# A weight stage in which each product waits for its own loads, and the first rows of x join it

## The reference

```
Q, K = x @ W_Q.T, x @ W_K.T;  invQ, invK = Q @ W_inv.T, K @ W_inv.T
xV  = einsum('btd,kdr->btkr', Q_side, V)          # forward: Q, V_fwd; inverse: invQ, W_inv_exp
yW  = einsum('btd,kdr->btkr', K_side, W)          # forward: K, W_fwd; inverse: invK, V_inv
h   = gelu(Q_side @ router_w1.T + router_b1);  weights = softmax(h @ router_w2.T + ...)
out = einsum('btkr,kdr->btd', xV * cumsum(yW) * weights, U) + weights @ b;  (fwd + alpha * inv) @ W_O.T
```

## Time and profile before

| | us |
|---|---|
| median of 3 runs | 2596.01 |
| the three runs | 2595.65, 2611.66, 2596.01 |
| profiled execution, its time | 2596.03 |
| profiled execution, its span | 2594.4 |
| PE busy, share of the span | 2275.7, 88% |
| DVE busy | 1828.6, 70% |
| ACT busy | 1465.8, 56% |
| first product on PE starts at | 27.67 |

### The profile page before, as it was taken

One profiled execution on the slowest core, in us unless ns is written; L12 is line 12 of the kernel. 1 busy time (PEld: TensorE's weight loads), 2 busy tenths in 40 slices (PEclk: granted clock), 3 DMA queues, 4 the chain that ended last, 5 costly groups with the idle time before them and its releaser, 6 DMA issues. The chain is left out here.

```text
span 2594.4 us, 45262 instructions
## 1 busy us (share of the span) xinstructions
PE 2275.7 (88%) x15192; PEld 1266.4 (49%) x15192; DVE 1828.6 (70%) x3199; ACT 1465.8 (56%) x2211; POOL 442.8 (17%) x647
## 2 busy tenths in 40 slices
PE   4678589999999999999999999859999967799988
PEld 3456233333333333333333333238888856555568
DVE  2554689999999999999999999313333356677936
ACT  2343167777777777777777777722222222255643
POOL 0000000000000000000000000013333310255645
PEclk9799589999999999999999999979999989576989
DMA  3666900220400403204004000042332259956465
GB/s 118 217 245 238 119 11 3 32 33 7 60 3 12 54 5 41 25 5 61 3 12 54 5 12 5 3 118 66 85 109 74 65 181 356 161 123 133 103 176 163
DMA packets 179609, 213.86 MB, mean 82 GB/s; under 512 B 71808, under 2 KB 121856, under 8 KB 176576
## 3 DMA queue, kind: packets, MB, share of 16 engines
q1 hardware_dynamic: 166576, 192.90, 30.2%
q10 hardware_dynamic: 7152, 13.84, 2.7%
q0 software_dynamic: 5728, 5.00, 0.9%
HBM read 121.41 MB, written 88.87 MB: 81 GB/s over the span
## 5 line engine op out<-in xcount | busy, mean ns | idle before, releaser
L931 DVE TENSOR_REDUCE a_maxes<-a_ps_a 128x2 f32<-128x1024 f32 x1024 | 1201.5, 1221 | 110.5 <-PE a_ps_a L1045 106.6
L996 ACT ACTIVATE a_prob<-a_ps_s 128x512 f32<-128x512 f32 (+1 forms) x1376 | 1035.7, 804 | 365.0 <-PE a_ps_s L1071 359.1
L1071 PE MATMUL a_ps_s<-a_Q,a_K 50*128 50x512 f32 x2048 | 593.9, 453 | 91.2 <-ACT a_prob L996 89.7
L1045 PE MATMUL a_ps_a<-a_K,a_Q 48*128 48x512 f32 x2048 | 550.8, 454 | 28.6 <-DMA a_Q<-s_halves 14.0
L1083 PE MATMUL a_ps_o<-a_prob,a_V 128*17 128x512 f32 x4096 | 540.9, 600 | 0.1
L1071 PEld LDWEIGHTS a_ps_s<-a_Q,a_K 50*128 50x128 f32 x2048 | 277.1, 185 | 508.5 <-ACT a_prob L996 457.9
L1045 PEld LDWEIGHTS a_ps_a<-a_K,a_Q 48*128 48x128 f32 x2048 | 245.2, 189 | 232.6 <-issue 104.9
L889 POOL DMA_DIRECT2D a_Q<-a_m_parts x128 | 64.3, 502 | 1282.7 <-DVE a_m_parts L923 1279.1
L1475 ACT ACTIVATE a_prob<-a_ps_s 128x512 f32<-128x512 f32 (+1 forms) x256 | 136.0, 583 | 134.1 <-PE a_ps_s L1566 131.0
L1416 DVE CUSTOM_DVE_ANT_0 a_scratch<-a_ps_a,k_mask 128x256 f32<-128x256 f32 (+1 forms) x512 | 177.4, 412 | 46.1 <-PE a_ps_a L1530 45.9
L1530 PE MATMUL a_ps_a<-a_K,a_Q 48*128 48x256 f32 (+1 forms) x512 | 128.5, 379 | 31.5 <-DMA a_Q<-s_halves 30.5
(11 more groups left out here) (177 smaller groups left out, 2327.6 us busy)
## 6 DMA issues: line engine op xcount, KB each, us to landing
s_halves<-p_parts SPq DMA_DIRECT2D x64, 512.0 KB, 5.0
s_xT<-p_xT SPq DMA_DIRECT2D x64, 256.0 KB, 4.3
c_xT<-s_xT SPq DMA_DIRECT2D x64, 256.0 KB, 4.8
a_K<-s_halves SPq DMA_DIRECT2D x63, 256.0 KB, 6.7
a_Q<-s_halves SPq DMA_DIRECT2D x186, 64.0 KB, 9.9
s_v<-p_v_out SPq DMA_DIRECT2D x16, 544.0 KB, 4.2
s_cT<-p_cT SPq DMA_DIRECT2D x32, 256.0 KB, 3.5
c_cT<-s_cT SPq DMA_DIRECT2D x32, 256.0 KB, 5.1
```

What stands on the lines that cost most here:

```text
L931: nc.vector.tensor_reduce(maxes[:, :, slot, qt, kc], ps_a[:, o:o + 2 * CH].rearrange("p (z k) -> p z k", z=2), AX.X, ALU.max).then_inc(a_d ...
L996: nc.scalar.activation(prob[:, ring:ring + len(t), :].rearrange("p r q -> p (r q)"), ps_s[:, bank:bank + len(t) * CH], ACT.Exp, scale=scal ...
L1045: last = nc.tensor.matmul(ps_a[:, o + side * CH:o + (side + 1) * CH], Q[rows, q0:q0 + P], K[rows, k0:k0 + CH], start=True, stop=True)
L1071: last = nc.tensor.matmul(ps_s[:, bank + x * CH:bank + (x + 1) * CH], K[rows, k0:k0 + P], Q[rows, q0:q0 + CH], start=True, stop=True)
```

## The change

The loads are put in eleven groups with a semaphore each, in another order, and the two first chunks of x (batch 0 and 1) are put between them. PE waits for the group of each product; the router's two products are made first. The plain splits are placed between the products' splits by a table, `PLAIN_AT`. The statistics of both chunks, the inverse roots and the normalising of the first are done in the weight stage; for this the buffers of the rows (`row_buffers`) live in a scope of their own around it and the projection of layer 0, and in one around that of layer 1, each closed by clearing its semaphores and a barrier. `row_statistics`, `inverse_root` and `normalise_rows` are the nested functions of `phase_project` word for word, moved out and given the buffers. What follows in layer 0 begins with the transposes.

```diff
@@ phase_weights
+        loads = {
+            "inverse": [(square["WinvT"][:], "W_invT"), (square["WQ"][:], "W_Q"), (square["WK"][:], "W_K")],
+            "router": [(square["W1T"][:], "router_w1T")],
+            "Vf": [(wide["Vf"][:], "V_fwd")], "Vi": [(wide["Vi"][:], "W_inv_exp")],
+            "qkv0": [(raw_qkv[:, 0], "w_qkvT_0")],
+            "Wf": [(wide["Wf"][:], "W_fwd")], "Wi": [(wide["Wi"][:], "V_inv")],
+            "o0": [(raw_o[:, 0], "w_oT_0")],
+            "out": [(square["WOT"][:], "W_OT"), (wide["Uf"][:], "U_fwd"), (wide["Ui"][:], "U_inv"),
+                    (bT[:, :, 0:E], "b_fwdT"), (bT[:, :, E:2 * E], "b_invT")],
+            "qkv1": [(raw_qkv[:, 1], "w_qkv_1")],
+            "last": [(raw_o[:, 1], "w_out_1"), (raw_g[:, :, 0:E1], "gateT"),
+                     (raw_g[:, :, E1:E1 + E1 * R1], "lora_UT"), (raw_g[:, :, E1 + E1 * R1:], "weightT"),
+                     (raw_v[:], "lora_V"), (W["w2"][:], "router_w2T")],
+        }
+        loaded = {g: n.sem(f"{g}_loaded") for g in loads}
...
+        base = E1 + E1 * R1
+        plain = [("qkv0", lambda part: W["qkv0"][:, part], raw_qkv[:, 0], 1.0),
+                 ("o0", lambda part: W["o0"][:, part], raw_o[:, 0], 1.0),
+                 ("qkv1", lambda part: W["qkv1"][:, part], raw_qkv[:, 1], 1.0),
+                 ("last", lambda part: W["o1"][:, part], raw_o[:, 1], 1.0),
+                 ("last", lambda part: W["gate"][:, part, :, 0:base], raw_g[:, :, 0:base], 1.0),
+                 ("last", lambda part: W["gate"][:, part, :, base:], raw_g[:, :, base:], 0.5),
+                 ("last", lambda part: W["loraV"][:, part], raw_v[:], 1.0)]
+        PLAIN_AT = {4: (0,), 8: (1,), 11: (2,), 13: (3, 4, 5, 6)}
...
-            for dst, src, k in loads:
-                sp.dma_start(dst, src.rearrange("(k p) n -> p k n", p=P)).then_inc(loaded, DMA)
+            for g, group in loads.items():
+                for dst, key in group:
+                    sp.dma_start(dst, I[key].rearrange("(k p) n -> p k n", p=P)).then_inc(loaded[g], DMA)
+                if g in ("router", "Vi"):
+                    load_rows(sp, L, I["x"], 0, 0 if g == "router" else 1)
...
+            def plain_high_part(i):
+                g, dst, src, factor = plain[i]
+                act.wait_ge(loaded[g], DMA * len(loads[g]))
+                nc.scalar.activation(dst(0), src, ACT.Copy, scale=factor).then_inc(plain_high, 1)
...
                 dst = split_target(W, j)
...
+                for i in PLAIN_AT.get(j, ()):
+                    plain_high_part(i)
...
-            act.wait_ge(loaded, DMA * n_loads)
-            for dst, src, factor in plain_splits(W, raw_qkv, raw_o, raw_g, raw_v):
-                nc.scalar.activation(dst(0), src, ACT.Copy, scale=factor).then_inc(high, 1)
...
-            pe.wait_ge(loaded, DMA * n_loads)
+            def have(g):
+                pe.wait_ge(loaded[g], DMA * len(loads[g]))
+            have("inverse")
...
+            have("router")
             j = 0
+            for t in range(DK):
+                for r, left in enumerate((WQ, WIQ)):
+                    for k in range(DK):
+                        o = (2 + j % 6) * CH + r * D
+                        last = nc.tensor.matmul(bank[:, o:o + D], left[:, k, t * P:(t + 1) * P],
+                                                square["W1T"][:, k, :], start=(k == 0),
+                                                stop=(k == DK - 1), skip_group_check=True)
+                last.then_inc(product, 1)
+                j += 1
             for left, right in ((WQ, "Vf"), (WIQ, "Vi"), (WK, "Wf"), (WIK, "Wi")):
...
+                have(right)
                 for t in range(DK):
...
+            have("out")
...
+            def plain_low_part(i):
+                g, dst, src, factor = plain[i]
+                dve.wait_ge(plain_high, i + 1)
+                nc.vector.scalar_tensor_tensor(dst(1), src, factor, f32(dst(0)), ALU.mult, ALU.subtract
+                                               ).then_inc(plain_low, 1)
+            row_statistics(nc, dve, L, 0, 0, passed)
             for j in range(N_SPLIT):
                 dve.wait_ge(high, 3 + j)
                 dst = split_target(W, j)
                 nc.vector.tensor_tensor(dst(1), bank[:, (2 + j % 6) * CH:(3 + j % 6) * CH], f32(dst(0)),
                                         ALU.subtract).then_inc(low, 1)
-            for i, (dst, src, factor) in enumerate(plain_splits(W, raw_qkv, raw_o, raw_g, raw_v)):
-                dve.wait_ge(high, 4 + N_SPLIT + i)
-                nc.vector.scalar_tensor_tensor(dst(1), src, factor, f32(dst(0)), ALU.mult, ALU.subtract
-                                               ).then_inc(low, 1)
+                for i in PLAIN_AT.get(j, ()):
+                    plain_low_part(i)
+                if j == 1:
+                    row_statistics(nc, dve, L, 0, 1, passed)
+                if j == 2:
+                    normalise_rows(nc, dve, L, 0, 0)
...
            dve.wait_ge(drawn, N_DRAWN)
...
+            dve.wait_ge(rows_loaded, DMA * len(rows))
...
+            for u in range(2):
+                inverse_root(pool, W, L, u, u)
...
+def row_buffers(n):
+    L = {"xn": n.sb("xn", [P, 2, TT, D]), "stats": n.sb("stats", [P, 2, TT, 6]),
+         "mean_var": n.sb("mean_var", [P, 2, TT, 2]), "var_eps": n.sb("var_eps", [P, 2, TT]),
+         "rstd": n.sb("rstd", [P, 2, TT]), "x_loaded": [n.sem(f"x_loaded{u}") for u in range(2)]}
+    for name in ("stat", "eps_ready", "rstd_ready", "xn_ready"):
+        L[name] = n.sem(name)
+    return L
+def load_rows(sp, L, x_dram, i, u):
+    sp.dma_start(L["xn"][:, u], x_dram[u, ds(i * CH, CH), :].rearrange("(t p) d -> p t d", p=P)
+                 ).then_inc(L["x_loaded"][u], DMA)
+def row_statistics(nc, dve, L, i, u, passed):
...
+def inverse_root(pool, W, L, c, u):
...
+def normalise_rows(nc, dve, L, i, u):
...
@@ phase_project
-            load(sp, 0, 0)
-            load(sp, 0, 1)
+            if not first:
+                load(sp, 0, 0)
+                load(sp, 0, 1)
...
-            statistics(0, 0)
-            statistics(0, 1)
-            normalise(0, 0)
+            if not first:
+                row_statistics(nc, dve, L, 0, 0, passed)
+                row_statistics(nc, dve, L, 0, 1, passed)
+                normalise_rows(nc, dve, L, 0, 0)
...
@@ recurrent_blocks
-            phase_weights(nc, W, I)
-            phase_project(nc, W, S, I["x"], 0)
+            with ExitStack() as first_projection:
+                L = row_buffers(Names(nc, first_projection, "l0"))
+                phase_weights(nc, W, I, L)
+                phase_project(nc, W, S, L, I["x"], 0)
             phase_attend_full(nc, W, S)
             phase_combine_experts(nc, W, S, I["x"], S["x1"])
-        phase_project(nc, W, S, S["x1"], 1)
+        with ExitStack() as second_projection:
+            L = row_buffers(Names(nc, second_projection, "l1"))
+            phase_project(nc, W, S, L, S["x1"], 1)
```

120 lines of the change are left out of this document (39 added, 81 removed).

## The result

| us | before | changed |
|---|---|---|
| median of the runs on one chip | 2595.83 (4 runs, 2589.51 to 2611.66) | 2563.43 (4 runs, 2549.81 to 2594.64) |
| all runs of this study | mean 2595.4, median 2596.8, deviation 9.9 (39 runs) | mean 2561.7, median 2558.8, deviation 12.8 (16 runs) |
| first product on PE starts | 27.67 | 8.36 |
| weight stage ends | 67.81 | 43.92 |
| first transpose | 78.47 | 45.08 |

The ratio is 0.9858 [0.9814, 0.9902]: the kernel is faster by 1.4%. That the two agree so closely is partly luck: a single run lies 10 to 13 us off its mean.

A forecast was written before the change was run, and what follows sets the result against it. PE, near 9 tenths busy through full attention, bounds the kernel, so the weight stage, where it waited 27.7 us for loads, only moves the start. -19.7 - 5.4 - 9.7 + 1.0 = -33.8 from 2596.03 gives 2562.2; range 2554 to 2574.

The forecast's parts named there:

- The first product: Weight stage: PE's first product waits for three loads only, starting at 8.0 instead of 27.67 us; gain 19.7 (17.2 to 21.3).
- The page's fit: Trainium skill's estimate for one transfer, 2 us plus bytes at 436 GB/s: first three loads there near 4.7 us; not adopted.
- Group waits, splits and rows, at 0: Weight stage: later load groups arrive in time, and splits and rows of x fit between the products; cost 0.
- The rival of starving products: Weight stage: real group waits make PE stand and run at half clock; gain falls to 8, 2588 us; 6%.
- the one of loads that don't land in the order of issue: Weight stage: Vf's group lands with the crowd near 30 us; gain 21.2, 2575 us; 7%.
- The margins: Weight stage: time between a group's landing and PE's need of it; smallest 5.7 us, for Vf.
- The tail: Weight stage's end: less work stays behind the last product, so it ends at 62.42, not 67.81; gain 5.4 us (4.5 to 5.8).
- The head: Start of the next stage: rows of x already normalised, so PE transposes when the barrier opens; gain 9.7 us (8.5 to 9.8).
- Barriers: End of each projection: one more clear and barrier, 0.5 us each, +1.0 in all (0.8 to 1.7).
- a run's own scatter: Range of the total: 2 us or so for this, plus shifts of the projection's clock dips, widened the forecast case to 2554 to 2570.
- the attention takes a different time from its first key load to its end: Full attention: one of the listed signs that the prediction is wrong; PE clock there was expected unchanged.
- the slower rival: Attention's opening: PE's clock rises later, 9.3 us lost per 10 us of such work; about 2655 us for 100 us; 4%.

The follow-up runs named there:

- experiment 5: Changed kernel with ACT issuing its ten rows of biases only after the three first loads have landed; 2571.15 us, 0.9889 of the kernel before.
- experiment 3: Changed kernel with the first rows of x loaded, counted and normalised in the projection again; 2568.2 us, 0.9899 of the kernel before.
- its repeats: The changed kernel run again unedited, twice; 2557.5 us (0.9875 of the kernel before) and 2558.93 us (0.9866).
- experiments 8 and 9: Changed kernel with extra PE products: 8, doubled score products in full attention's tail, 2557.48 us; 9, products on old operands before band attention's query waits, 2561.85 us.
- experiments 4: Changed kernel with the rows' semaphores cleared together with the projection's, one scope less; 2552.97 us, 0.9843 of the kernel before.

## Why the prediction was right

**The first product.** 8.0 was forecast, with 6.4 and 10.5 as ends; it came at 8.36, and at 7.5 in the mean of six traces. The gain is 19.3 to 20.2, the term said 19.7. SP's queue had moved 0.74 MB by 6 us and 1.04 by 8 us, so the rows of the queue in the earlier trace rows carried over. The page's fit (4.7 us) was too early by 3 us; even with the biases away the earliest is 5.68.

**Group waits, splits and rows, at 0.** Shown twice: 24.40 us for the products before and after, and no wait of PE on a load behind the first. The rival of starving products is out, and so is the one of loads that don't land in the order of issue: every group is there when PE needs it. The margins were somewhat smaller than worked out: the first rows of x landed at 13.3, where the forecast said 10.7 (10.2 by its own rates; and 24.1, not 24.7, for the out group).

**The inverses.** From the first product to the router's it takes 7.17 us in place of 6.48. The second group of eight takes 2.91 where it took 2.22. This is the execution's and not the change's: the other five traces with the same start have 5.93, 6.78, 6.87, 6.42 and 5.97, and the second trace of the kernel before has 7.46. What differs is when, within the second group, the products speed up. The granted clock doesn't show it: it reads 1.00 from 8.3 us on, though the first eight products take 0.47 us each, near the 0.52 of those at 0.50 in experiment 5, and those of the router 0.26.

**The tail.** From the last drain to the stage's end 43.92 - 39.93 = 3.99; 3.87 had been put together from `o1` and the rows from 65.24 to 67.81. With the start 0.36 later, the inverses 0.7 and the tail 0.12, the stage ended 1.2 after the 42.7 of the forecast; in the mean of the six traces it ended at 42.4.

**The head.** 1.16 us from stage end to transpose, a gain of 9.5; 9.7 in experiment 3. The transposes fell to the half clock, as reckoned, and `p_carry` at 47.58 came just before the low part at 47.85. It fits with 0.2 us to spare.

**Barriers.** +1.0 was taken, 0.5 for each of two; they cost 0.4 and nothing visible.

**The sum at the marks.** Five traces share the first 230 us of the changed kernel (it, its repeats, experiments 8 and 9). Their first transposes come at 45.1, 42.4, 43.4, 44.0 and 42.9, mean 43.6, against 78.5 and 79.3 before: -35.3, where the terms say -34.8. From there to the full attention they take 190.5 in the mean against 191.6: -1.0, where +0.5 was taken for the barrier. So at the start of the attention, the gain is **36.3** (234.1 against 270.4), 2 more than forecast. At DVE's last maximum it is 33.5 (1608.6 against 1642.1), since the clock rises later in the attention's opening. Two misses of opposite sign, +2 and -2.8 us, leave the total where it had been put: that part of the agreement is luck. The projection's 1.5 us are less than its own spread (188.5 to 192.0), and no run tells whether they are the clock's dips or the earlier stores.

**What failed.** The step of the range that put "a run's own scatter" at "2 us or so". It is 9.9 us before and 12.8 after, and of the four runs of the first comparison one, 2594.64, lay 20 us above the range and one, 2549.81, 4 us below. The three runs shown (one of them 15.6 us up) would have said so; the text mentioned that run and didn't use it. A second one is "the attention takes a different time from its first key load to its end", a sign of being wrong that came true. The forecast put nothing for it. In the opening of the full attention the clock rose 5 to 13 us later behind its start than before, in all five traces, and that cost 2.8 us: the slower rival's own mechanism, at a small size. Whether the change brings it isn't shown; in experiments 4 and 5, which have the change, it rises at 68 us as before. The larger losses by the same mechanism, PE at half clock with much work, lie where the rival did not look: in that stage's tail, in four of the ten unfilled traces with the change and in neither of the two before, and in the band attention, in both kernels. They cost up to 14 us in the one and 24 in the other (262.1 against the 238.0 of the first repeat). One run against one could have given anything from 20 us slower (2574.25 against 2594.64) to 68 us faster (2612.39 against 2544.31).

## What to carry to other kernels

Ahead of a bound engine's first work, ask which loads that work needs and wait for these alone, in the order of use; check the later groups by bytes ahead over the queue's measured rate. Keep transfers of many small packets out of the first microseconds, and put them on a queue whose engine has nothing else to do. Where a kernel's single runs scatter, look for stretches of half clock before ranking edits of a few microseconds, and compare marks of the trace ahead of them.
